# Cross-attention with a ternary feed-forward: where the maxima's unread output is written

## The reference

```python
x = x + xattn(layernorm(x), ctx, ctx, mask, Wq, bq, Wk, bk, Wv, bv, Wo, bo)
x = x + ffn(layernorm(x), w1, w2)

# xattn: q, k, v = x @ W + b, split into heads
scores = einsum('bhqd,bhkd->bhqk', q, k) / sqrt(8)
scores = where(mask == 0, -1e9, scores)
out = einsum('bhqk,bhkd->bhqd', softmax(scores), v)      # then @ Wo + bo

# ffn: h = gelu(bitlinear(x, w1)); return bitlinear(h, w2)
# bitlinear: activations rounded to 8 bits by row, weights to -1, 0, 1
```

## Time and profile before

| | |
|---|---|
| median of three runs | 934.4 us (931.29, 934.4, 935.69) |
| profiled execution | 931.15 us, its span 929.4 us |
| PE busy | 851.8 us, 92% |
| DVE busy | 785.6 us, 85% |
| ACT busy | 705.8 us, 76% |
| POOL busy | 305.7 us, 33% |
| L1190, the reduction | 768 of 705 ns, 502.7 us |
| L1190, the accumulator read | 768 of 141 ns |

### The profile page before, as it was taken

How to read it: one execution, slowest core, us unless ns; L and a number is a source line. 1 busy time by engine, 2 the same in 40 slices (tenths; PEclk the granted TensorE clock), 3 DMA queues, 4 the chain that set the end, 5 groups by cost and what they waited for, 6 DMA issues and landing times.

```text
span 929.4 us, 33993 instructions
## 1 busy us (share of the span) xinstructions
PE 851.8 (92%) x11724; PEld 639.2 (69%) x11724; DVE 785.6 (85%) x2597; ACT 705.8 (76%) x1272; POOL 305.7 (33%) x360
## 2 busy tenths in 40 slices
PE   3567889999999999999999999999999999999983
PEld 2254667777777777777777777777777777777672
DVE  4588578899898989899898989898898989998954
ACT  2445558979787888979787888979787888978672
POOL 8330242333333332333333332333333332323300
PEclk9589899999999999999999999999999999999997
DMA  5541123333233333333233333343233323340100
GB/s 135 120 107 48 38 61 97 87 90 86 67 89 82 90 88 96 84 98 84 64 89 82 88 87 95 84 101 84 65 89 82 88 83 95 87 106 23 37 2 6
DMA packets 78990, 74.01 MB, mean 80 GB/s; under 512 B 10240, under 2 KB 75248, under 8 KB 78960
## 3 DMA queue, kind: packets, MB, share of 16 engines
q1 hardware_dynamic: 77167, 72.78, 30.6%
q10 hardware_dynamic: 1793, 0.83, 0.3%
HBM read 47.97 MB, written 0.92 MB: 53 GB/s over the span
## 4 chain that ended last, share of the span: by engine, by line
PE 41%; DVE 26%; issue 19%; ACT 6%; SPq 2%; DMA 2%; DVEq 2%; POOL 0%; ACTq 0%; POOLq 0%
DVE ps_p L1190 11%; PE ps_p L836 6%; PE ps_v L952 6%; PE ps_p L832 5%; PE ps_p L890 5%; PE ps_p L905 5%; DVE seg_max L1190 4%; PE ps_p L829 4%; PE ps_p L918 3%; PE ps_p L911 3%; ACT L696 2%; ACT L729 2%; ACT probs L729 2%; DMA ctx_sb<-in_ctx_dram 1%; DVE row_stat L1014 1%
## 5 line engine op out<-in xcount | busy, mean ns | idle before, releaser
L1190 DVE CUSTOM_DVE_ANT_0 ps_p<-ps_p,mask_bias 120x500 f32<-120x500 f32 x768 | 502.7, 705 | 46.7 <-PE ps_p L890 30.2
L729 ACT ACTIVATE probs<-ps_p 125x448 f32<-125x448 f32 x768 | 356.4, 557 | 66.3 <-PE ps_p L918 63.7
L639 POOL TENSOR_TENSOR k_lo<-k_full,keys 128x500 fp32r<-128x500 f32 x96 | 127.5, 1328 | 249.3 <-ACT keys L719 244.7
L905 PE MATMUL ps_p<-qry_lo,keys 64*125 64x448 f32 x768 | 162.5, 418 | 13.7 <-ACT probs L729 4.4
L890 PE MATMUL ps_p<-keys,qry_hi 64*120 64x500 f32 x768 | 162.5, 443 | 11.5 <-DMA keys<-k_lo 6.0
L952 PEld LDWEIGHTS ps_v<-probs,vals 125*32 125x32 f32 x6144 | 145.1, 110 | 22.8 <-issue 22.6
L952 PE MATMUL ps_v<-probs,vals 125*32 125x112 f32 x6144 | 160.5, 260 | 0.3 <-ACT probs L729 0.3
L911 PEld LDWEIGHTS ps_p<-qry_hi,keys 64*125 64x125 f32 x1536 | 146.3, 184 | 8.8
L918 PE MATMUL ps_p<-own_query,mask_bias 57*125 57x448 f32 x768 | 145.0, 371 | 5.1 <-DMA own_query<-shift 5.1
L911 PE MATMUL ps_p<-qry_hi,keys 64*125 64x224 f32 x1536 | 146.0, 267 | 0.0
L905 PEld LDWEIGHTS ps_p<-qry_lo,keys 64*125 64x125 f32 x768 | 72.6, 182 | 69.4 <-DVE seg_max L1190 32.1
(11 more groups left out here) (125 smaller groups left out, 857.7 us busy)
## 6 DMA issues: line engine op xcount, KB each, us to landing
keys<-k_lo SPq DMA_DIRECT2D x384, 62.5 KB, 2.0
ctx_sb<-in_ctx_dram SPq DMA_DIRECT2D x31, 750.0 KB
mask_sb<-in_mask_Bx1xSxS_ik_dram SPq DMA_DIRECT2D x64, 328.1 KB
own_query<-shift SPq DMA_DIRECT2D x64, 1.8 KB
out_dram<-x_rows SPq DMA_DIRECT2D x16, 56.0 KB, 1.6
ctx_sb<-in_ctx_dram ACTq DMA_DIRECT2D x1, 750.0 KB
x_rows<-in_x_dram SPq DMA_DIRECT2D x1, 672.0 KB, 11.0
w_sb<-in_L_ffn_w_dram SPq DMA_DIRECT2D x2, 256.0 KB, 8.5
```

Of the source, the lines that this page charges most:

```text
L639: pool.tensor_tensor(k_lo[:, (p + n) % 2, :], k_full[:, (p + n) % 2, :], keys[:, p, 0, at].bitcast(F32), ALU.subtract)\
L729: act.activation(probs[:, (c + NG * p) % NP, h], ps_p[0:KC, BANK[how]["S", c, h], 0:HC], ACT.Exp)\
L905: pe.matmul(score_bank(c, h, how), keys[rows, p, 0, at], qry_lo[rows, p, :, :], start=True, stop=False, skip_group_check=True)
L1190: dve.tensor_tensor_reduce(ps_p[0:MROWS, BANK[how][slot], 0:SEG], ps_p[0:MROWS, BANK[how][slot], 0:SEG], mask_bias[0:MROWS, p, s * SEG:(s ...
```

## The change

The output of the reductions that nobody reads gets another place. `xn` and `xnt` become views of one tile, `spare`, of their joint size. From the loop's first turn on, the sums of all reductions are written in bf16 into a view of `spare` (`max_junk`, one strip of 500 for each bank). In "lead", where `xn` and `xnt` are in use and `probs` is not yet, they go into a view of `probs` (`early_junk`). In "first_even" and "first_odd" both are in use, and the sums go back into their bank as before.

```diff
-        xn = sb("xn", [PAIR, 2, 4, D])
+        spare = sb("spare", [128, 2 * 4 * (D + PAIR)])
+        xn = spare[0:PAIR, 0:2 * 4 * D].rearrange("p (a r d) -> p a r d", a=2, d=D)
         xn_stat = sb("xn_stat", [PAIR, 12, 4])
-        xnt = sb("xnt", [D, 2, 4 * PAIR])
+        xnt = spare[:, 2 * 4 * D:].rearrange("p (a n) -> p a n", a=2)
...
         probs = sb("probs", [KC, NP, 2, HC])
+        early_junk = probs[:].rearrange("p n h c -> p (n h c)").bitcast(BF16)[0:MROWS, 0:NBANK * SEG]\
+            .rearrange("p (b k) -> p b k", b=NBANK)
+        max_junk = spare[:].bitcast(BF16)[0:MROWS, 0:NBANK * SEG].rearrange("p (b k) -> p b k", b=NBANK)
...
                 dve.sem_inc(seg_begun, 1)
-                dve.tensor_tensor_reduce(ps_p[0:MROWS, BANK[how][slot], 0:SEG],
+                if how == "lead":
+                    junk = early_junk[:, BANK[how][slot], :]
+                elif how in ("first_even", "first_odd"):
+                    junk = ps_p[0:MROWS, BANK[how][slot], 0:SEG]
+                else:
+                    junk = max_junk[:, BANK[how][slot], :]
+                dve.tensor_tensor_reduce(junk,
                                          ps_p[0:MROWS, BANK[how][slot], 0:SEG],
                                          mask_bias[0:MROWS, p, s * SEG:(s + 1) * SEG].bitcast(F32), 1.0, LOWEST,
```

## The result

The changed kernel takes 921.35 us (median of four runs, 919.49 to 922.84) against 933.89 before (median of four, 931.29 to 935.69): ratio 0.9857, 95% interval 0.9831 to 0.9883. It is faster by 12.5 us, outside the range I gave. Its profiled execution took 920.87 us, the span 919.1.

What follows compares the result with a forecast made beforehand. PE was taken to set the pace, with DVE close behind. DVE's 0 and ACT's -0.4 us made the profiled 931.15 into 930.75; put on the median, 934.4 - 0.4 = 934.0 us, range 924 to 940.

Steps and rivals of the forecast that it cites:

- What bounds it: Main loop: PE sets the pace, busy 51.05 of about 52 us a turn; DVE, 46.65, sometimes holds it up.
- The share of 28%: Maxima pairs: 138.5 of about 492 us lie on the chain; used to turn DVE time into kernel time.
- The stream: Reduction's 500 elements: 0.51 us whichever memory receives them; a narrower output was worth 0.
- the fixed part: Reduction into PSUM 0.08 us against addition into SBUF 0.07: a PSUM destination costs at most 0.01 us more.
- the tail: End of an instruction past its successor's start: 0.08 us for both the reduction and the addition, so alike.
- Behind an accumulator read: Reduction takes 0.64 us there instead of 0.59; the 0.05 was read as accumulator still in use, so 0 gain.
- the reciprocal: L1151, also writing PSUM: 0.90 us behind an accumulator read and behind an idle stretch, taken as evidence against a PSUM cost.
- Release of the bank: `seg_done` rises on the accumulator read, ending 0.14 us after its start in both versions; the bank comes free no earlier.
- Rival A: Reductions' PSUM output, or turning from SBUF to PSUM, costs 0.05 us a pair; removal saves 10 us: 924; chance 0.19.
- The rule: Skill page's PSUM source cost extended to destinations: 65 ns a reduction, 13 us of the kernel, time near 921.
- Rival B: Reductions' SBUF output meets POOL there, 0.3 us per POOL instruction, 25 us in all: 959; chance 0.13.
- ACT's part: Exponentials' PSUM reads beside the maxima speed up: bounds 0 and -0.8 us, taken as -0.4.

Runs made afterwards that it cites:

- experiment 2: Changed kernel with the first 12 reductions of each batch writing sums into PSUM, the last 12 into SBUF: 925.42 us, ratio 0.9902 to the kernel before.
- experiment 5: Changed kernel with even reductions' sums in PSUM and maxima in SBUF, odd ones the reverse: 927.76 us, ratio 0.992 to the kernel before.
- experiment 1: Changed kernel with every second reduction writing its sums back into PSUM, the others into SBUF: 924.1 us, ratio 0.9884 to the kernel before.
- experiment 4: Changed kernel with sums and accumulator reads both written into the PSUM bank from the loop on: 922.67 us, ratio 0.9864 to the kernel before.
- experiment 3: Changed kernel with sums still in SBUF but accumulator reads written into PSUM from the loop on: 937.25 us, ratio 1.0024 to the kernel before.
- experiment 7: Changed kernel with sums of banks 0 to 2 in SBUF as f32, bank 3 SBUF bf16, banks 4 to 6 PSUM: 923.88 us, profiled execution only.

## Why the prediction was wrong

- **What bounds it** was right: PE sets the pace and is held up now and then by the maxima. The share of 28% came out near: the pace gained at most 48 x 0.04 = 1.9 us of DVE in a turn, and the turn gained 0.52 from it, 27%. That is partly luck, since pairs are not all worth the same (experiment 2).
- **The stream, the fixed part and the tail** were read rightly: 0.59 us behind an ordinary instruction is what the changed kernel still has. They were no test of a change, though: the addition followed a read that also wrote SBUF, and ahead of the reduction at 431.92 the copy of L1167 had ended its writing by 432.00, early enough for a change to hide by the estimate under "Two theories".
- **Behind an accumulator read** is the step that failed: I took 0 for DVE, and DVE is busy 23 us less. I had the 0.05 us in hand, named the turn from SBUF to PSUM as a possible cause, and put it aside because of the reciprocal. The runs show 0.04 us a pair that go with the change of memory, worth 0.52 us a turn or 7.5 us of the kernel (experiment 5). The reciprocal is a poor control: it writes 112 elements in 0.86 us, so its writing may well begin late enough to hide a change. That was not tried. The reductions themselves show the cost to go when a neighbour writes the same memory (experiments 1, 4 and 5), while the accumulator is used the same way.
- **Release of the bank** failed by the same cause. I took the read's 141 ns for the instruction's own time. 58 of them were the change from PSUM to SBUF, a wait that no view lists as one. It did come earlier, and with the earlier `turn_max` that is worth 0.28 us a turn, some 4 us, or 5.7 by the whole times, where I had 0.
- **Rival A** was the case, in the second of its two mechanisms ("a turn from writing SBUF to writing PSUM") and with its sign in the profile: 0.60 us in `spare` and 0.63 in `ps_p` in one run. Its price of 10 us, beside the 12.5 measured, is near by luck: it took 0.05 instead of 0.04 us for the pace and left out the earlier end of the reads. It foresaw fewer microseconds of waits for `seg_max`; these hardly changed (32.9, 25.5 and 9.0 us now against the earlier trace rows), and the gain is seen in PE's idle time instead.
- **The rule** I set against the row gave 921, the measured time, by luck: it was my extension to destinations. The Trainium skill's "VectorE: DVE Perf Modes", section "The TRN2 errata", lists for VectorE one fixed cost from SBUF to SBUF and a larger one from PSUM to SBUF, and none for a PSUM destination. Experiment 4 has both outputs of each pair in PSUM and runs at 922.67 us, so a price of the PSUM destination is not what this kernel paid.
- **Rival B** did not occur: the longest reduction into `spare` takes 681 ns beside a median of 673, though POOL is busy a third of the time.
- **ACT's part** of at most 0.8 us stays open, for it is smaller than the noise. Nothing speaks for it: the exponentials take 559 ns in the mean against 557 before, and experiment 4, which writes the sums to PSUM again, has all the gain.

## What to carry to other kernels

When instructions of DVE that follow each other without a wait alternate between PSUM and SBUF outputs, and one of them is short, compare its duration with the same kind of instruction elsewhere: the read-out of one element that took 141 ns here was 83 ns of work and a wait. Put the unread output, or the small result, into the memory that the neighbour writes. And before a row serves as control, work out whether the cost in question could hide in it.

## What the runs showed of the hardware

An accumulator read ended later when it wrote to the other memory than the reduction ahead of it: by 58 ns from PSUM to SBUF (141 ns in the kernel before, 83 in the changed one) and by 49 ns from SBUF to PSUM (141 in experiment 3, 92 in experiment 4). The next reduction was late, by some 0.04 us, only where both the read and it changed the memory. It was not where only the read did (experiment 5) or only the reduction did (experiment 1). That the second change hides where enough time lies between the two writes is the estimate above; the profile shows no single write. Where nothing changes, PSUM and SBUF destinations give the same pace, 0.60 us for 500 elements and the read (experiment 4 and the changed kernel), and in SBUF f32 and bf16 do too (experiment 7). Whether other pairs of instructions pay the same was not tried.
